# A 32-group fused attention and state-space kernel: the calls of every engine's loop in another order

## The chip, the cores and the metric

The kernel runs on one core of one Trainium2 chip. The metric is the time of one execution on the device in microseconds (us), given as the median of several runs. One further execution was taken with the profiler; all rows below come from that one.

## What is computed

The input is x and a context, 64 sequences of 128 positions by 256 features each, in f32. Three layers follow one another for each sequence:

```python
# 1: attention with 16 heads of 16, queries masked, then add and layernorm
q, k, v = relu(x @ Wq + bq), relu(ctx @ Wk + bk), relu(ctx @ Wv + bv)
x = layernorm(softmax(where(m, q @ k.T / 4, 1e-9)) @ v + x) * gamma + beta
# 2: a state-space block, 8 heads of 64, state 128, a causal convolution of 4 taps
z, xBC, dt = split(rms(x) @ in_proj_w); xBC = silu(conv(xBC)); dt = softplus(dt + dt_bias)
h = h * exp(dt * A) + (dt * xh) B.T;  y = h @ C + D_skip * xh      # a scan over the positions
x = x + rms(y * silu(z)) @ out_proj_w
# 3: cross attention on the same context, 8 heads of 32, then the residual
x = x + (softmax(where(pad, -1e9, layernorm(x) @ Wq1 @ (ctx @ Wk1).T / sqrt(32))) @ (ctx @ Wv1)) @ Wo
```

The state-space part is done as a masked matrix product within each sequence: the scan forms the decay matrix L, TensorE forms C times B, and y is XH times L.

## The kernel before, in words

Two sequences (b = 0, 1) make a group g; there are 32 groups. The program is written engine by engine. Each engine has a set of small helper functions, one for each step of the work of a group, and a loop over s in which they are called in an order that is written out by hand. A call such as cp(s - 3, 0) works on group s - 3 and does nothing when that group does not exist, so the loop is a software pipeline: up to six groups are in flight on one engine. Semaphores join the engines; every helper waits for the counts that it needs, and an engine runs its list strictly in order. The calls on VectorE, ScalarE and GpSimd count their own iterations: only the order on each engine matters, not that s has the same value.

PSUM has eight banks (tiles called bank). The table USES lists in which order TensorE's calls use which bank; the function bank() finds from it what the call must wait for, which is the reader of the last use of that bank.

TensorE's calls (lines 286 to 696) are of three sorts. **Full-array products** take all 128 rows and columns. The projections q, k, v, cp (six of them), z are single-pass products of a value split in a high and a low part (helper proj3, line 294; v in L330, L335); k1, q1 (L535), v1 (L573), o (L522, L523) and wp (L635) are two-record f32 products; gm is L486, dp L445. **Transposes** by the identity: nt, ht, ot, bx, tC (helper turn, L397), tn (L367), bd (L456). **Part-array products** use a part of the rows or columns and stand four (or two) to the array: sA (L354), sT (L387, closed by four products L391) and sC (L593, L597) take 32 rows; av (L411, 8 records a call) and oC (L622, 16 records a call) take 32 columns, y (L508, 16 records a call) 64 columns.

What the steps of a group do, in their order: ScalarE's split_x and split_c and GpSimd's lo_x and lo_c (L1453, L1458) split the inputs; q, k, v, with the results copied out by qe, ke, ve on ScalarE and masked by qm on GpSimd. sA gives the scores for the row maxima (mA on VectorE, L707; nm, L719 and L721), tn and nt_ turn them, sT forms the scores again, transposed, with the maxima subtracted, eA (ScalarE, L1188) takes the exponential, av applies it to V, oa copies, ot transposes, rc and xo (VectorE) divide, xr (GpSimd) adds x. The layernorm is bs, bg, xs, x2 on VectorE with the power rs (L1482) on GpSimd. The rms norm of the second layer is n1 (ScalarE), nr (GpSimd, a power, L1491), nx (ScalarE); nt, nh, nl transpose and split it. dp, d0, de, dc, dq, dd, da, bd, dk form the step sizes and decays; dk's result goes to a DRAM scratch and comes back spread over the partitions (dec_out and dec_in on SyncE, tile DB). cp, ac, tap (L848), th, xc make the convolution; z, zt, sz the gate; bx, xhe, xd and dx the operands; gm the product of C and B. scan (VectorE, L872) makes L out of DB, lg (L881) multiplies it by gm's result, y multiplies by XH, yd (L900) adds; ga (GpSimd, L1518), qq, s2_ gate and square; o projects out, r1 and r2 (a power, L1533), hh (L917) norm and add. hs, hg (L930), hr (GpSimd, a power, L1542), hm (VectorE, L937), hx (ScalarE, L1224, tile xh) are the next layernorm, ht (L397, bank from xh) transposes its result, q1 and k1 project, sC, mC, eC, rC, nC, tC, pC, oC, oT, wp and fin are the cross attention and the last residual. L, SZ, XH, DX, SQ, OA and Q1T are single tiles, the others rings of 2 to 5.

SyncE issues all transfers of the loop, in order, with waits of its own: the loads of a coming group, the decay round trip and the store of a finished one. Four late weight loads, and on VectorE and GpSimd the preparation of the second layer's weights (late(), later()), are put into an early iteration.

## Time and profile before

| | |
|---|---|
| median of 3 runs | 1472.45 us (1471.77 to 1473.89) |
| the profiled execution | 1475.54 us, from its first to its last instruction 1473.7 |
| mean granted TensorE clock in it | 0.979 |
| busy: TensorE, VectorE, ScalarE, GpSimd | 1379.9, 1238.6, 1097.1, 922.4 us |
| instructions | 42007, of them 15112 matrix products |

Busy time is the time in which an engine executes anything. Products on TensorE overlap, so that the distance between the starts of two products is what each costs, not the duration of one; the ends are modelled. A row of the timeline may merge instructions of the same line that follow one another; the brackets give the idle time before it and who ended it. "issue" means that nothing the profile shows was waited for.

### The profile page before, as it was taken

What the parts mean: (1) busy time and instruction counts of PE and PEld (TensorE: products, weight loads), DVE (VectorE), ACT (ScalarE), POOL (GpSimd) and SP (SyncE); (2) the same over time, 40 slices, a digit from 0 to 9 for tenths busy, and PEclk for the clock granted to TensorE, in tenths of its full rate; (3) what the DMA queues carried; (4) which work ended last, traced back from release to release, by engine and by line L of the source; (5) the groups of instructions that cost most, each with busy time, mean ns of one, the idle gap of its engine ahead of it and who ended that gap; (6) DMA issues with size and microseconds to landing.
All of it is one profiled execution on the core that took longest, in us unless ns stands there. A gap on an engine that the chain in (4) does not pass through costs nothing. (4 is left out here: it accounts for less than half of the span.)

```text
span 1473.7 us, 42007 instructions
## 1 busy us (share of the span) xinstructions
PE 1379.9 (94%) x15112; PEld 1175.2 (80%) x15112; DVE 1238.6 (84%) x3050; ACT 1097.1 (74%) x3300; POOL 922.4 (63%) x1125
## 2 busy tenths in 40 slices
...
DMA packets 41132, 86.91 MB, mean 59 GB/s; under 512 B 5728, under 2 KB 10976, under 8 KB 40928
## 3 DMA queue, kind: packets, MB, share of 16 engines
...
q14 instruction: 81, 0.66, 0.1%
...
## 5 line engine op out<-in xcount | busy, mean ns | idle before, releaser
L848 DVE SCALAR_TENSOR_TENSOR ACC<-bank,cw,ACC 128x250 f32<-128x250 f32 (+2 forms) x576 | 271.2, 472 | 25.2 <-ACT ACC L1278 19.2
L1518 POOL TENSOR_TENSOR Y<-Y,SZ 128x512 f32<-128x512 f32 x64 | 140.6, 2197 | 202.2 <-DVE Y L900 202.2
L294 PE MATMUL bank<-xnT,wnl 128*128 128x256 f32 x640 | 202.1, 316 | 1.5 <-ACT PC L1351 0.7
L1188 ACT ACTIVATE PTA<-bank 128x512 f32<-128x512 f32 x256 | 136.3, 603 | 80.1 <-PE bank L391 80.1
L1351 ACT ACTIVATE PC<-bank,stc 128x128 f32<-128x128 f32 x512 | 183.0, 415 | 7.3 <-DVE stc L957 4.8
L294 PE MATMUL bank<-xnL,wnh 128*128 128x256 f32 x640 | 179.5, 280 | 0.0
L294 PE MATMUL bank<-xnT,wnh 128*128 128x256 f32 x640 | 179.3, 280 | 0.0
L707 DVE TENSOR_REDUCE sta<-bank 128x4 f32<-128x512 f32 x256 | 165.7, 679 | 4.2 <-PE bank L354 4.2
L872 DVE TENSOR_TENSOR_SCAN L<-DB,id 128x1024 f32<-128x1024 f32 x64 | 146.1, 2283 | 0.0
L294 PEld LDWEIGHTS bank<-xnT,wnl 128*128 128x128 f32 x640 | 121.0, 189 | 29.4 <-issue 26.2
L1548 POOL TENSOR_TENSOR PC<-PC,stc 128x512 f32<-128x512 f32 x128 | 133.3, 1042 | 10.3 <-DVE stc L964 10.3
L1351 ACT ACTIVATION_READ_ACCUMULATOR PC<-bank,stc 128x1 f32 x512 | 130.6, 255 | 0.0
L1278 ACT ACTIVATE ACC<-bank,cw 128x256 f32<-128x256 f32 x192 | 111.6, 581 | 20.6 <-PE bank L294 19.6
L522 PE MATMUL bank<-wout,Y 128*128 128x256 f32 x512 | 122.5, 382 | 1.9 <-POOL SQ L1526 1.9
L294 PEld LDWEIGHTS bank<-xnL,wnh 128*128 128x128 f32 x640 | 121.6, 190 | 0.0
L294 PEld LDWEIGHTS bank<-xnT,wnh 128*128 128x128 f32 x640 | 121.1, 189 | 0.0
L1363 ACT ACTIVATE PTC<-bank 128x512 f32<-128x512 f32 x128 | 77.7, 609 | 55.9 <-PE bank L397 52.7
L522 PEld LDWEIGHTS bank<-wout,Y 128*128 128x128 f32 x512 | 95.4, 191 | 14.4 <-issue 2.3
L957 DVE TENSOR_REDUCE stc<-bank 128x4 f32<-128x512 f32 x128 | 82.1, 683 | 16.8 <-PE bank L597 16.8
L387 PE MATMUL bank<-QT,KT 32*128 32x128 f32 x2048 | 77.7, 289 | 19.7 <-DVE sta L707 10.0
L937 DVE SCALAR_TENSOR_TENSOR stb<-stb 128x1 f32<-128x1 f32 x64 | 35.6, 557 | 71.5 <-POOL stb L1542 71.5
L1491 POOL TENSOR_TENSOR stn<-stn,mhalf 128x1 f32<-128x1 f32 x64 | 91.6, 1430 | 5.3
...
## 6 DMA issues: line engine op xcount, KB each, us to landing
...
```

Of the source, the lines that this page charges most:

```text
L294: mm = e.matmul(t[:, c0:c0 + T], wt[:, k, m:m + 128], x[:, k, :], start=(n == 0), stop=(n == 5))
L522: e.matmul(t[:, 0:256], Y[b][:, kk * 128:(kk + 1) * 128], wout[:, kk, :], start=(kk == 0), stop=(kk == 3))
L707: e.tensor_reduce(sta[ns % 4][:, 4 * j:4 * j + 4], t[:, :].rearrange("p (i k) -> p i k", i=4), AX_X, ALU.max, negate=True).then_inc(s_mA, 1)
L848: e.scalar_tensor_tensor(out=w, in0=t[:, 0:T].rearrange("p (b t) -> p b t", b=NB)[:, :, 0:125 + k], scalar=cw[:, c, k:k + 1], in1=w, op0=A ...
L872: e.tensor_tensor_scan(L[:, :, :].rearrange("p h t -> p (h t)"), DB[b][:, :], id8[:, :, :].rearrange("p h t -> p (h t)"), 0.0, ALU.mult, A ...
L957: e.tensor_reduce(stc[g % 4][:, 4 * i:4 * i + 4], t[:, :].rearrange("p (i k) -> p i k", i=4), AX_X, ALU.max, negate=True).then_inc(s_mC, 1)
L1188: e.activation(PTA[n % 4][:, :, :], t[:, :].rearrange("p (i k) -> p i k", i=4), ACT.Exp).then_inc(s_eA, 1)
L1278: e.activation(ACC[n % 3][:, :, :], t[:, 0:T].rearrange("p (b t) -> p b t", b=NB), ACT.Identity, bias=cw[:, c, 4:5], scale=cw[:, c, 3:4]). ...
L1351: op = e.activation(PC[n % 5][:, p, :], t[:, p * 128:(p + 1) * 128], ACT.Exp, bias=stc[g % 4][:, 4 * i + p:4 * i + p + 1], accum_out=stc[g ...
L1491: e.tensor_tensor(w, w, mhalf[:, :], ALU.pow).then_inc(s_nr, 1)
L1518: e.tensor_tensor(cv(Y[b][:, :]), cv(Y[b][:, :]), SZ[:, :, b * 128:(b + 1) * 128], ALU.mult).then_inc(s_ga, 1)
L1548: e.tensor_tensor(PC[n % 5][:, :, :], PC[n % 5][:, :, :], stc[g % 4][:, 16 + 4 * i:20 + 4 * i].unsqueeze(2).to_broadcast([128, 4, 128]), A ...
```

## The change

The calls of all five loops are put into another order, with other distances between groups, and the bank of every use is assigned anew. No helper function is changed, and every group has the same instructions as before. The loop has two iterations more, of which the first four give TensorE no work. The late weight loads are issued in iteration 6 instead of 4 of SyncE's list, and late() on VectorE runs in iteration 5 instead of 2 of its list; on GpSimd late() and later() stay in iterations 1 and 2. In the diff, the calls of an iteration are written side by side, with nothing left out but the middle of USES.

```diff
 USES = [
-    (("tn", 0, 2), 4), (("nt", 0, 3), 6), (("ht", 1, 5), 7), (("y", 0, 4), 3), (("sT", 0, 2), 4), (("sT", 1, 2), 7),
...
+    (("sT", 0, 6), 3), (("sT", 1, 6), 7), (("sT", 2, 6), 4), (("sT", 3, 6), 0), (("y", 1, 8), 2), (("tC", 3, 9), 3),
...
 ]
-STEPS = NG + 9
+STEPS = NG + 11
@@ the calls of one iteration, sync @@
-                if s == 4:
+                if s == 6:
-dec_in(s-7, 1) dec_in(s-7, 0) load_m(s-4) load_c(s-4) store(s-9) load_u(s-6) load_t(s-5) load_x(s-3)
-dec_out(s-6)
+load_t(s-7) dec_in(s-9, 1) load_x(s-5) load_c(s-5) dec_out(s-8) store(s-11) load_m(s-5) load_u(s-7)
+dec_in(s-8, 0)
@@ the calls of one iteration, tensor @@
-tn(s-2, 0) nt(s-3, 0) ht(s-5, 1) y(s-4, 0) sT(s-2, 0) q1(s-5, 0) q1(s-5, 1) bx(s-4, 1) gm(s-4, 1) dp(s-3, 0)
-tn(s-2, 1) sC(s-5, 0) av(s-2, 0) av(s-2, 1) av(s-2, 2) cp(s-3, 0) y(s-4, 1) cp(s-3, 1) av(s-2, 3) k1(s-3, 0)
-k1(s-3, 1) o(s-4, 0) tC(s-5, 0) q(s-1, 0) ot(s-2, 0) cp(s-3, 2) sT(s-2, 1) cp(s-3, 3) bd(s-3, 0) cp(s-3, 4)
-q(s-1, 1) z(s-3, 0) av(s-2, 4) av(s-2, 5) av(s-2, 6) tC(s-5, 1) av(s-2, 7) cp(s-3, 5) tC(s-5, 2) k(s-1, 0)
-ot(s-2, 1) k(s-1, 1) o(s-4, 1) sA(s-1, 0) tC(s-5, 3) z(s-3, 1) oC(s-5, 0) oC(s-5, 1) v(s-1, 0) bx(s-3, 0)
-sA(s-1, 1) v1(s-3, 0) ht(s-4, 0) gm(s-3, 0) wp(s-5, 0)
+sT(s-6, 0) y(s-8, 1) tC(s-9, 3) cp(s-7, 0) dp(s-7, 0) q(s-5, 1) cp(s-7, 1) av(s-6, 0) av(s-6, 1) oC(s-9, 0)
+av(s-6, 2) oC(s-9, 1) av(s-6, 3) tn(s-6, 1) o(s-8, 1) ot(s-6, 0) cp(s-7, 2) ht(s-8, 0) cp(s-7, 3) sT(s-6, 1)
+bd(s-7, 0) cp(s-7, 4) z(s-7, 0) av(s-6, 4) av(s-6, 5) av(s-6, 6) av(s-6, 7) ht(s-8, 1) cp(s-7, 5) q1(s-8, 0)
+q1(s-8, 1) ot(s-6, 1) k1(s-6, 0) sC(s-8, 0) wp(s-9, 0) v(s-5, 0) bx(s-7, 0) k1(s-6, 1) gm(s-7, 0) tC(s-8, 0)
+z(s-7, 1) sA(s-5, 0) y(s-7, 0) tC(s-8, 1) k(s-4, 0) k(s-4, 1) q(s-4, 0) sA(s-5, 1) bx(s-7, 1) tC(s-8, 2)
+tn(s-5, 0) v1(s-6, 0) gm(s-7, 1) nt(s-6, 0) o(s-7, 0)
@@ the calls of one iteration, vector @@
-                if s == 2:
+                if s == 5:
-mA(s-2, 4) hm(s-5, 1) lg(s-4, 0) fin(s-6, 0) mA(s-2, 5) mA(s-2, 6) mA(s-2, 7) nl(s-3, 0) nl(s-3, 1) nm(s-2,
-1) yd(s-4, 0) scan(s-4, 1) lg(s-4, 1) d0(s-3, 0) d0(s-3, 1) mC(s-5, 0) mC(s-5, 1) mC(s-5, 2) dc(s-3, 0)
-dc(s-3, 1) dc(s-3, 2) yd(s-4, 1) tap(s-3, 0) rC(s-5, 0) dc(s-3, 3) dc(s-3, 4) mC(s-5, 3) tap(s-3, 1) dc(s-3,
-5) dc(s-3, 6) rC(s-5, 1) dc(s-3, 7) dc(s-3, 8) tap(s-3, 2) dc(s-3, 9) dc(s-3, 10) kk1(s-3, 0) kk1(s-3, 1)
-tap(s-3, 3) r1(s-4, 0) tap(s-3, 4) rC(s-5, 2) dc(s-3, 11) hh(s-4, 0) rc(s-2, 0) xc(s-3, 0) rC(s-5, 3)
-tap(s-3, 5) xo(s-2, 0) tap(s-3, 6) tap(s-3, 7) xc(s-3, 1) dk(s-3, 0) bs(s-2, 0) bg(s-2, 0) tap(s-3, 8)
-xs(s-2, 0) tap(s-3, 9) hs(s-4, 0) tap(s-3, 10) tap(s-3, 11) xc(s-3, 2) x2(s-2, 0) sz(s-3, 0) hg(s-4, 0)
-xc(s-3, 3) tap(s-3, 12) tap(s-3, 13) tap(s-3, 14) tap(s-3, 15) rc(s-2, 1) xo(s-2, 1) tap(s-3, 16) tap(s-3,
-17) xc(s-3, 4) hm(s-4, 0) bs(s-2, 1) bg(s-2, 1) r1(s-4, 1) xs(s-2, 1) xc(s-3, 5) hh(s-4, 1) mA(s-1, 0)
-hs(s-4, 1) mA(s-1, 1) hg(s-4, 1) x2(s-2, 1) mA(s-1, 2) mA(s-1, 3) sz(s-3, 1) scan(s-3, 0) nm(s-1, 0)
+dc(s-6, 2) tap(s-6, 3) tap(s-6, 4) tap(s-6, 5) xc(s-6, 0) dc(s-6, 3) dc(s-6, 4) dc(s-6, 5) hm(s-7, 0)
+dc(s-6, 6) dc(s-6, 7) r1(s-7, 1) dc(s-6, 8) dc(s-6, 9) dc(s-6, 10) xc(s-6, 1) hh(s-7, 1) rc(s-5, 0) hs(s-7,
+1) hg(s-7, 1) dc(s-6, 11) xo(s-5, 0) tap(s-6, 6) tap(s-6, 7) hm(s-7, 1) dk(s-6, 0) tap(s-6, 8) tap(s-6, 9)
+bs(s-5, 0) bg(s-5, 0) tap(s-6, 10) xs(s-5, 0) tap(s-6, 11) xc(s-6, 2) tap(s-6, 12) x2(s-5, 0) tap(s-6, 13)
+tap(s-6, 14) sz(s-6, 0) xc(s-6, 3) tap(s-6, 15) tap(s-6, 16) tap(s-6, 17) xc(s-6, 4) rc(s-5, 1) xo(s-5, 1)
+xc(s-6, 5) mC(s-7, 0) mC(s-7, 1) kk1(s-5, 0) mC(s-7, 2) fin(s-8, 0) rC(s-7, 0) scan(s-6, 0) rC(s-7, 1)
+lg(s-6, 0) mC(s-7, 3) kk1(s-5, 1) rC(s-7, 2) bs(s-5, 1) sz(s-6, 1) bg(s-5, 1) mA(s-4, 0) mA(s-4, 1) mA(s-4,
+2) yd(s-6, 0) xs(s-5, 1) mA(s-4, 3) x2(s-5, 1) nm(s-4, 0) mA(s-4, 4) mA(s-4, 5) mA(s-4, 6) mA(s-4, 7)
+rC(s-7, 3) scan(s-6, 1) lg(s-6, 1) r1(s-6, 0) nl(s-5, 0) nl(s-5, 1) nm(s-4, 1) yd(s-6, 1) hh(s-6, 0) hs(s-6,
+0) hg(s-6, 0) d0(s-5, 0) d0(s-5, 1) tap(s-5, 0) tap(s-5, 1) tap(s-5, 2) dc(s-5, 0) dc(s-5, 1)
@@ the calls of one iteration, scalar @@
-pC(s-6, 0) qe(s-2, 0) da(s-4, 0) ac(s-4, 2) th(s-4, 1) eA(s-3, 4) eA(s-3, 5) eA(s-3, 6) ac(s-4, 3) eA(s-3,
-7) ac(s-4, 4) th(s-4, 2) qq(s-5, 1) zt(s-4, 0) th(s-4, 3) qe(s-2, 1) pC(s-6, 1) oa(s-3, 1) pC(s-6, 2)
-ac(s-4, 5) th(s-4, 4) ke(s-2, 0) ke(s-2, 1) th(s-4, 5) hx(s-5, 0) pC(s-6, 3) split_x(s-1) zt(s-4, 1) oT(s-6,
-0) n1(s-3, 0) n1(s-3, 1) ve(s-2, 0) xhe(s-4, 0) nx(s-3, 0) split_c(s-1) he(s-5, 0) nx(s-3, 1) v1e(s-4, 0)
-hx(s-5, 1) nt_(s-2, 0) he(s-5, 1) nh(s-3, 0) nh(s-3, 1) eA(s-2, 0) eA(s-2, 1) eA(s-2, 2) eA(s-2, 3) q1e(s-5,
-0) q1e(s-5, 1) xhe(s-4, 1) nt_(s-2, 1) de(s-3, 0) de(s-3, 1) qq(s-4, 0) de(s-3, 2) eC(s-5, 0) ac(s-3, 0)
-dq(s-3, 0) eC(s-5, 1) oa(s-2, 0) ac(s-3, 1) eC(s-5, 2) eC(s-5, 3) th(s-3, 0) dd(s-3, 0)
+de(s-7, 2) ac(s-7, 1) qe(s-5, 1) dq(s-7, 0) th(s-7, 0) oT(s-9, 0) oa(s-6, 0) th(s-7, 1) v1e(s-7, 0) hx(s-8,
+0) nt_(s-6, 1) dd(s-7, 0) he(s-8, 0) ac(s-7, 2) da(s-7, 0) split_x(s-4) ac(s-7, 3) eA(s-6, 4) eA(s-6, 5)
+eA(s-6, 6) hx(s-8, 1) eA(s-6, 7) th(s-7, 2) ac(s-7, 4) he(s-8, 1) zt(s-7, 0) th(s-7, 3) oa(s-6, 1) ac(s-7,
+5) q1e(s-8, 0) q1e(s-8, 1) th(s-7, 4) n1(s-6, 0) th(s-7, 5) eC(s-8, 0) eC(s-8, 1) xhe(s-7, 0) ve(s-5, 0)
+eC(s-8, 2) split_c(s-4) zt(s-7, 1) eC(s-8, 3) nx(s-6, 0) pC(s-8, 0) pC(s-8, 1) ke(s-4, 0) ke(s-4, 1) qe(s-4,
+0) n1(s-6, 1) qq(s-7, 0) nt_(s-5, 0) nx(s-6, 1) xhe(s-7, 1) pC(s-8, 2) nh(s-6, 0) nh(s-6, 1) eA(s-5, 0)
+eA(s-5, 1) pC(s-8, 3) eA(s-5, 2) ac(s-6, 0) eA(s-5, 3) qq(s-7, 1) de(s-6, 0) de(s-6, 1)
@@ the calls of one iteration, gpsimd @@
-dx(s-3, 0) xr(s-2, 1) r2(s-4, 1) rs(s-2, 1) nr(s-2, 0) nr(s-2, 1) lo_x(s) hr(s-4, 1) xd(s-3, 0) ga(s-3, 0)
-xd(s-3, 1) dx(s-3, 1) s2_(s-3, 0) ga(s-3, 1) nC(s-4, 0) lo_c(s) nC(s-4, 1) r2(s-3, 0) nC(s-4, 2) xr(s-1, 0)
-rs(s-1, 0) s2_(s-3, 1) qm(s, 0) nC(s-4, 3) qm(s, 1) hr(s-3, 0)
+qm(s-1, 0) r2(s-4, 1) qm(s-1, 1) hr(s-4, 1) xr(s-2, 0) rs(s-2, 0) nr(s-2, 0) dx(s-3, 0) xr(s-2, 1) nC(s-4,
+0) xd(s-3, 0) nC(s-4, 1) lo_c(s) lo_x(s) nC(s-4, 2) rs(s-2, 1) ga(s-3, 0) nr(s-2, 1) s2_(s-3, 0) xd(s-3, 1)
+nC(s-4, 3) dx(s-3, 1) r2(s-3, 0) ga(s-3, 1) hr(s-3, 0) s2_(s-3, 1)
```

## Rows read from the trace of the kernel before

**Rows 1.** The page: its first line and TensorE's busy time.

```profile
span 1473.7 us, 42007 instructions
...
PE 1379.9 (94%) x15112; PEld 1175.2 (80%) x15112; DVE 1238.6 (84%) x3050; ACT 1097.1 (74%) x3300; POOL 922.4 (63%) x1125
```

**Rows 2.** Busy time by window: core, window, length, then each engine busy (instructions), clock, DMA share.

```profile
0.00:72.00 72.00, 38.83 (x359) 30.79 (x360) 36.21 (x82) 25.86 (x63) 32.75 (x57) 0.76 0.32 102
700.00:743.50 43.50, 42.18 (x474) 36.12 (x473) 37.94 (x95) 34.10 (x104) 28.29 (x35) 1.00 0.19 60
1403.00:1473.70 70.70, 54.08 (x441) 42.71 (x441) 39.06 (x98) 41.94 (x150) 34.73 (x41) 0.88 0.08 27
```

**Rows 3.** TensorE's timeline: start, busy, line, tiles, count, idle time before.

```profile
715.26 0.86 PE L411 MATMUL bank<-PTA,V 128*32 128x128 f32 x24
716.05 0.39 PE L294 MATMUL bank<-xnT,wnl 128*128 128x256 f32 x1
716.28 0.28 PE L294 MATMUL bank<-xnL,wnh 128*128 128x256 f32 x1
716.40 0.28 PE L294 MATMUL bank<-xnT,wnh 128*128 128x256 f32 x1
...
716.75 0.28 PE L294 MATMUL bank<-xnT,wnh 128*128 128x256 f32 x1
716.96 1.09 PE L508 MATMUL bank<-L,XH 128*64 128x128 f32 x16
...
718.86 0.43 PE L411 MATMUL bank<-PTA,V 128*32 128x128 f32 x8
719.22 1.99 PE L535 MATMUL bank<-cU,wk 128*128 128x256 f32 x8
...
731.30 0.66 PE L397 MATMUL bank<-ident,PC 128*128 128x128 f32 x4
731.89 0.42 PE L411 MATMUL bank<-PTA,V 128*32 128x128 f32 x8
...
740.43 1.08 PE L622 MATMUL bank<-PTC,V 128*32 128x128 f32 x32
741.44 0.50 PE L330 MATMUL bank<-vbias,onesr 128*128 128x512 f32 x1
```

**Rows 4.** TensorE's timeline, where it is idle in that step.

```profile
706.89 0.41 PE L397 MATMUL bank<-ident,xh 128*128 128x128 f32 x2 [0.90 <-ACT xh L1224]
...
708.79 1.12 PE L387 MATMUL bank<-QT,KT 32*128 32x128 f32 x29 [0.41 <-issue]
```

**Rows 5.** VectorE's timeline of the same step.

```profile
699.48 2.28 DVE L872 TENSOR_TENSOR_SCAN L<-DB,id 128x1024 f32<-128x1024 f32 x1
...
705.06 0.99 DVE L937 SCALAR_TENSOR_TENSOR stb<-stb 128x1 f32<-128x1 f32 x1 [2.42 <-POOL stb L1542]
...
707.70 1.87 DVE L707 TENSOR_REDUCE sta<-bank 128x4 f32<-128x512 f32 x3
...
713.45 1.22 DVE L881 TENSOR_TENSOR L<-L,bank 128x1024 f32<-128x1024 f32 x1
...
737.16 0.15 DVE L937 SCALAR_TENSOR_TENSOR stb<-stb 128x1 f32<-128x1 f32 x1
...
743.01 2.28 DVE L872 TENSOR_TENSOR_SCAN L<-DB,id 128x1024 f32<-128x1024 f32 x1
```

**Rows 6.** The list of waits, the wait of L937.

```profile
DVE stb L937 <- POOL stb L1542: 71.5, 31, 3.0
```

**Rows 7.** GpSimd's timeline of the same step.

```profile
699.49 2.63 POOL L1491 TENSOR_TENSOR stn<-stn,mhalf 128x1 f32<-128x1 f32 x1
...
704.16 0.21 POOL L1540 TENSOR_SCALAR stb<-stb 128x1 f32<-128x1 f32 x1
704.46 0.57 POOL L1542 TENSOR_TENSOR stb<-stb,mhalf 128x1 f32<-128x1 f32 x1
704.99 1.04 POOL L1509 TENSOR_TENSOR XH<-XH,dtt 128x512 f32<-128x512 f32 x1
```

More of the change, by code:

```diff
@@ new lines, in tensor @@
+                av(s - 6, 3)
+                tn(s - 6, 1)
+                o(s - 8, 1)
+                ot(s - 6, 0)
+                cp(s - 7, 2)
+                ht(s - 8, 0)
+                cp(s - 7, 3)
+                sT(s - 6, 1)
+                bd(s - 7, 0)
+                cp(s - 7, 4)
+                z(s - 7, 0)
+                av(s - 6, 4)
+                av(s - 6, 5)
+                av(s - 6, 6)
+                av(s - 6, 7)
+                ht(s - 8, 1)
+                cp(s - 7, 5)
@@ new lines, in tensor @@
+                q1(s - 8, 0)
+                q1(s - 8, 1)
+                ot(s - 6, 1)
+                k1(s - 6, 0)
+                sC(s - 8, 0)
+                wp(s - 9, 0)
+                v(s - 5, 0)
+                bx(s - 7, 0)
+                k1(s - 6, 1)
+                gm(s - 7, 0)
+                tC(s - 8, 0)
+                z(s - 7, 1)
+                sA(s - 5, 0)
+                y(s - 7, 0)
+                tC(s - 8, 1)
+                k(s - 4, 0)
+                k(s - 4, 1)
@@ new lines, in vector @@
+                dc(s - 6, 4)
+                dc(s - 6, 5)
+                hm(s - 7, 0)
+                dc(s - 6, 6)
+                dc(s - 6, 7)
+                r1(s - 7, 1)
+                dc(s - 6, 8)
+                dc(s - 6, 9)
+                dc(s - 6, 10)
+                xc(s - 6, 1)
+                hh(s - 7, 1)
+                rc(s - 5, 0)
+                hs(s - 7, 1)
+                hg(s - 7, 1)
+                dc(s - 6, 11)
+                xo(s - 5, 0)
+                tap(s - 6, 6)
@@ new lines, in vector @@
+                tap(s - 6, 15)
+                tap(s - 6, 16)
+                tap(s - 6, 17)
+                xc(s - 6, 4)
+                rc(s - 5, 1)
+                xo(s - 5, 1)
+                xc(s - 6, 5)
+                mC(s - 7, 0)
+                mC(s - 7, 1)
+                kk1(s - 5, 0)
+                mC(s - 7, 2)
+                fin(s - 8, 0)
+                rC(s - 7, 0)
+                scan(s - 6, 0)
+                rC(s - 7, 1)
+                lg(s - 6, 0)
+                mC(s - 7, 3)
```

410 lines of the change are left out of this document (171 added, 239 removed), and 20 rows, old and new, of the table USES.

## The prediction

> **What bounds the kernel now.** I read the page first: TensorE is busy 1379.9 of 1473.7 us, 94%, and the engine after it, VectorE, 1238.6 us [rows 1]. Then one step of the loop: VectorE's first scan of a step starts at 699.48 and the next one at 743.01 [rows 5], so a step takes 43.5 us, and in a stretch of that length TensorE is busy 42.2, VectorE 37.9, ScalarE 34.1 and GpSimd 28.3 us at the full granted clock, 1.00 [rows 2]. Filling and draining take the first 72 us (38.8 busy) and the last 70.7 (54.1 busy) [rows 2]; the 1331 us between them hold the starts of some thirty steps. So TensorE's own list of work sets the step, plus whatever holds it up. Both parts are read from its timeline.
>
> TensorE's work contains something that busy time hides. The single-pass projections (L294) start 0.12 us apart (716.28 to 716.40). Where a part-array product stands before or after one, it is more: 0.21 from the last projection to the product (716.75 to 716.96), and 0.23 from the first projection behind it to the second (716.05 to 716.28). Eight part-array products alone between full ones take 0.36 us (718.86 to 719.22), but twenty-four in a row take 0.79 (715.26 to 716.05) [rows 3]: a further sixteen cost 0.43, eight of them 0.215. So a lone group costs 0.36 - 0.215 = 0.145 of its own, 0.09 at the full product ahead and 0.11 at the full product behind: **0.345 us for each separate run**. Where the neighbour is a transpose the way back is cheaper: four transposes between two such groups take 0.59 (731.30 to 731.89) against 4 x 0.11, so 0.15 for both sides of them together [rows 3].
>
> TensorE also waits at one place in each step: 0.90 us for ScalarE's xh (706.89), and, the queue then being empty, another 0.41 ahead of sT (708.79) [rows 4], 1.31 together. Followed back: VectorE's hm (L937) waits 2.42 us, 31 times [rows 5, 6]; it waits for the power at 704.46 on GpSimd, which stands there behind a power of 2.63 us, and takes 0.57 itself [rows 7], since GpSimd ran beside the scan that began at 699.48; and hm itself then takes 0.99 instead of 0.15 (737.16 [rows 5]), while GpSimd's multiplication of 704.99 runs beside it.
>
> **The change, part by part.**
>
> Part-array groups that stand together. Counting the 55 calls of a step, runs of part-array calls between full ones are ten before: {y0 sT0}, {sC av0-2}, {y1}, {av3}, {sT1}, {av4-6}, {av7}, {sA0}, {oC0 oC1}, {sA1}. After it seven: {sT0 y1}, {av0 av1 oC0 av2 oC1 av3}, {sT1}, {av4-7}, {sC}, {sA0 y0}, {sA1}. Priced: av3 joins, -0.345. av7 joins, and its neighbour was a transpose group: -0.30. oC joins av: oC alone takes 1.01 for thirty-two, of which 0.145 goes (740.43 to 741.44 [rows 3]), -0.345. y1 comes beside sT0 in place of y0, and y0 beside sA0: one run fewer, but the products are of different shapes and I let each keep its own 0.145, so only -0.20. sC is parted from av: +0.20. Sum **-0.99**. Moreover six of the seven runs are now followed by transposes (tC, tn, bd, ht, tC, bx) where eight of ten were followed by projections or the like: up to 5 x 0.055 = 0.27 more, of which I take 0.1, because a transpose just pays for a single product. Together 1.1 us a step (ends 0.8, if unlike shapes and alternating calls gain nothing, and 1.25), in all 32 groups: **-35 us**.
>
> The rule against this in the Trainium skill ("TensorE: Matmul & The Clock Gate", Part 3, The mechanism) is that a weight load overlaps with products in flight only when it goes to another row group; all the av and oC products use all rows, so by it each would wait for its own load and nothing would be gained by standing side by side; the step would lose only the waits. It is a rival below. The trace speaks against it: 0.027 us between starts in a row of av.
>
> The waits. In the new order VectorE has hm0 sixteen places behind hg0, across the loop's end, and hm1 five behind hg1: dc11, xo0, tap6, tap7 and then hm1, about 1.4 us, in which GpSimd needs 0.8 (0.21 and 0.57, rows 7) if it is free; and on GpSimd hr1 now stands fourth, no longer behind the powers of nr and lo_x. ht0 and ht1 on TensorE no longer stand together ahead of y: ht1 comes after av7, some 3.5 us behind sT1. So the 1.31 us should go. What is late next? I laid the new lists beside one another with the durations of the rows. The nearest ring: sA1 ends, VectorE does mA4 to mA7, rC3, scan1, lg1 (three mA in 1.87, scan 2.28, lg 1.22 [rows 5]: 6.1 us), then y1 may start; TensorE meanwhile has bx1, tC2, tn0, v1, gm1, nt, o0, sT0, 6.8 us. A margin of 0.5 after two crossings. Others (nt behind nx1, oT behind oC1, d0 behind dp) have 0 to 0.6. New waits are therefore between 0 and the old 1.31; I take 0.45, near zero since every margin that I can work out is positive, but not zero since they are small. Gain 0.86 us in the 29 full steps: **-25 us**. VectorE allows it: with its busy 37.9 and all its idle time except the 2.42 it would need at most 43.5 - 2.4 = 41.1 a step, against a TensorE step of 43.5 - 1.1 - 0.86 = 41.5.
>
> Edits with nothing to pay. Banks (USES): the same eight; the new place of each is covered by the margins above. SyncE: DMA engines are busy a fifth of the time [rows 2]; the decay transfer (dec_out, then dec_in 0) still starts behind dk and has some 11 us on VectorE's list until scan0; dec_in 1 is one iteration later but scan1 is 12 us behind scan0. If it were late, each microsecond would stand in front of scan and lg and soon of y. GpSimd: moved past its own power instructions, 28.3 busy, so there is room. The ends: two iterations more in the loop, but the first four are empty; from the first k to the last wp there are 4.8 steps against 4.6. The late weights (late on VectorE) come after the maxima instead of ahead of them, and late on GpSimd now stands before qm of group 0. I put that at 0, with 8 us either way.
>
> **The sum.** -35 - 25 = -60. The profiled execution took 1475.5 us (its span 1473.7 and some 1.8 around it), so 1415.5; the median of the runs shown is 3.1 lower, 1472.45, so **1413** for the median.
>
> **Rivals.**
> 1. *The waits form again at their old size.* The switches go (-35), but the rings catch TensorE as before, for 1.3 us a step: 1437. For it: several margins of a few tenths, VectorE at 37.9 of 42.4. Against: the one old wait has a clear cause that is gone.
> 2. *Joining gains nothing*, since each product pays for its own weights whatever stands beside it, or since gaps only move: the waits go, -25, 1447. The 0.215 against 0.36 speaks against it.
> 3. *Both fall away*, within 3 us of before: 1470 to 1475.
> 4. *Slower: GpSimd and VectorE block one another and VectorE becomes the bound.* Place: VectorE's hh, hm, x2 and bs, each behind a small power on GpSimd, with the two scans of a step. A power beside a scan took 2.1 us more than alone, and hm beside a multiplication 0.84 more [rows 5, 7]. These are eight places in a step. With its 41.1 (everything but the one wait) it loses to the old order as soon as these meetings add more than 2.4 us; two lost powers (4.2) less half a microsecond of cover each make the step 44.0, +0.5 x 31: 1488. Against: GpSimd has 13 us of room and the powers stand early in its list. The Trainium skill ("SBUF — State Buffer", Who interferes with whom) has the cause: a VectorE instruction with two SBUF inputs and a GpSimd one that reads SBUF exclude each other for the whole instruction. By that rule only the timing of the two lists counts, which no row of before shows for the new lists.
>
> **How the numbers follow.** The forecast, 1398 to 1430: 0.50. Better than that, with no new wait and the ends better: 0.05. Rival 1 (to 1450): 0.23. Rival 2: 0.05. Rival 3: 0.05. Rival 4: 0.12. A run of this kernel can be told from no change at about 0.2%, 3 us. Faster 0.83, same 0.05, slower 0.12. Low end: 1.25 x 32 + 1.31 x 29 + 6 at the ends = 84, 1389. The high end takes in rivals 1 and 2 and half of the way to 3: 1460; left out are 0.17.
>
> **What would show it.** Step: scan to scan 41.2 to 41.9 us. Switches: TensorE busy 1345 or so; the row av, av, oC, av, oC, av (64 products) in one piece of some 1.95 us with no step of 0.36; four to six transposes behind a run at 0.15 over their own time in all. Waits: the idle before ht, 26 us in total now, under 5; hm's wait for GpSimd under 15 us in total; new TensorE waits of under 0.5 us a step, first at y1 (for L) or nt (for xn). Wrong if: TensorE's busy time stays over 1370 (rival 2), if the busy time falls but waits of 1.3 us a step stand elsewhere (rival 1), or if VectorE is over 94% busy or waits for GpSimd over 2.4 us a step (rival 4). A longer stretch ahead of the first cp than 80 us would make the ends the step that failed.

## The result: 1428.5 us, 3.0% less, and the profile after

| | before | after |
|---|---|---|
| median, same chip | 1473.07 us | 1428.51 us (1427.62 to 1431.83) |
| ratio | | 0.9702, 95% interval 0.9684 to 0.9721 |
| first instruction to last, profiled | 1473.7 us | 1426.0 us |
| up to the first cp | 71.8 us | 58.5 us |
| 31 steps, first cp to last cp | 1331.3 us | 1294.4 us |
| behind the last cp | 70.6 us | 73.2 us |

The change makes the kernel 3% faster, inside the predicted range and 15 us above the predicted number. The last three lines are read from the starts of cp(…, 0) on TensorE (the expectations below put the first of them 0.2 to 0.3 us earlier): of the 47.7 us gained, 36.9 are in the steps and 10.8 at the two ends.

The page of after, its first line, busy times and the granted clock, against [rows 1]:

```profile
span 1426.0 us, 42008 instructions
...
PE 1329.9 (93%) x15112; PEld 1160.4 (81%) x15112; DVE 1267.2 (89%) x3050; ACT 1089.3 (76%) x3300; POOL 891.7 (63%) x1125
...
PEclk9999999999999999999999999999999999999997
```

Busy time by window of after (window, length, each engine busy with its count, clock, DMA share), one step and the fill, against [rows 2]:

```profile
700.00:741.84 41.84, 40.52 (x472) 35.55 (x471) 38.17 (x93) 33.23 (x101) 27.19 (x34) 1.00 0.21 60
0.00:36.00 36.00, 16.40 (x166) 13.53 (x167) 20.86 (x36) 14.02 (x31) 24.36 (x44) 1.00 0.57 188
36.00:77.00 41.00, 31.48 (x379) 25.07 (x378) 33.33 (x96) 25.14 (x66) 14.42 (x23) 1.00 0.14 44
```

The step shown takes 41.84 us (VectorE's scan0 at 704.88, then 746.7), not 43.5. It is one of the shorter ones: the middle steps take 41.8 to 43.0, 42.2 in the mean. TensorE is busy 40.52 of the 41.84, down from 42.18 of 43.50, and VectorE a little more. So the busy time fell as forecast, but 1.3 us of each step is idle still.

TensorE's timeline of after, the two waits of a step and the rows that the change made, against [rows 3, 4]:

```profile
699.53 1.10 PE L535 MATMUL bank<-cU,wk 128*128 128x256 f32 x4 [0.51 <-DMA cU<-in_cT]
...
706.62 0.39 PE L486 MATMUL bank<-XC 128*128 128x128 f32 x2
708.12 0.63 PE L397 MATMUL bank<-ident,PC 128*128 128x128 f32 x4 [1.11 <-POOL PC L1548]
...
727.30 0.64 PE L411 MATMUL bank<-PTA,V 128*32 128x128 f32 x16
727.76 0.62 PE L622 MATMUL bank<-PTC,V 128*32 128x128 f32 x16
728.20 0.40 PE L411 MATMUL bank<-PTA,V 128*32 128x128 f32 x8
728.42 0.62 PE L622 MATMUL bank<-PTC,V 128*32 128x128 f32 x16
728.86 0.40 PE L411 MATMUL bank<-PTA,V 128*32 128x128 f32 x8
729.19 0.33 PE L367 MATMUL bank<-ident,NM 128*128 128x128 f32 x1
```

The merged row (av, av, oC, av, oC, av: 64 products) takes 1.89 us from 727.30 to the transpose at 729.19, with no step of 0.36 in it. The old wait of 0.90 for xh is gone, and there are two new ones: 1.11 us at the transpose tC0 for GpSimd's normalised rows PC, and 0.51 at k1 for a transfer. The list of waits of after (engine, line, waited for: us in total, times, longest) says how often:

```profile
PE bank L397 <- POOL PC L1548: 36.1, 33, 2.1
...
PE bank L535 <- DMA cU<-in_cT: 5.1, 9, 1.2
...
PE bank L397 <- ACT xh L1224: 3.9, 2, 3.5
```

The wait at ht for xh was 26.3 us over the run and is 3.9 now, and hm's wait for GpSimd, 71.5 us [rows 6], is 2.1. The cause of the new wait is on the other two engines. VectorE's and GpSimd's timelines of after:

```profile
704.20 0.68 DVE L970 TENSOR_TENSOR X<-bank,X 128x512 f32<-128x512 f32 x1
704.80 0.17 DVE L964 RECIPROCAL stc<-stc 128x4 f32<-128x4 f32 x1
704.88 2.26 DVE L872 TENSOR_TENSOR_SCAN L<-DB,id 128x1024 f32<-128x1024 f32 x1
...
707.25 1.22 DVE L881 TENSOR_TENSOR L<-L,bank 128x1024 f32<-128x1024 f32 x1
```

```profile
705.05 2.93 POOL L1548 TENSOR_TENSOR PC<-PC,stc 128x512 f32<-128x512 f32 x1 [2.62 <-DVE stc L964]
...
708.94 1.03 POOL L1548 TENSOR_TENSOR PC<-PC,stc 128x512 f32<-128x512 f32 x1
```

rC0 (0.17 us, L964) gives GpSimd what nC0 needs, but the scan starts right behind it at 704.88, and nC0 at 705.05 then takes 2.93 us instead of the 1.03 of the next one. tC0 stands behind it. Over the whole run these multiplications took 1.49 us each where they had taken 1.04; the group of L1548 in before and in after (count, then busy time and mean ns of one, then the idle time before):

```profile
L1548 POOL TENSOR_TENSOR PC<-PC,stc 128x512 f32<-128x512 f32 x128 | 133.3, 1042 | 10.3 <-DVE stc L964 10.3
```

```profile
L1548 POOL TENSOR_TENSOR PC<-PC,stc 128x512 f32<-128x512 f32 x128 | 191.1, 1494 | 78.0 <-DVE stc L964 78.0
```

And the transfer: SyncE's timeline of after, and the chain of waits of after where it passes through:

```profile
692.90 0.32 SPq L256 DMA_DIRECT2D dec_scratch<-decT  x1
693.27 0.42 SPq L270 DMA_DIRECT2D out_x<-X  x1
693.74 0.43 SPq L250 DMA_DIRECT2D QM<-qm_rows  x1
694.60 0.33 SPq L244 DMA_DIRECT2D cU<-in_cT  x1
```

```profile
694.60 4.80 DMA cU<-in_cT
```

load_u stands behind dec_out, which waits for VectorE's dk, so cU is issued at 694.60 and lands 4.8 us later, at 699.40; k1 has by then waited 0.51. In some steps it waits up to 1.2 us, which is why the steps of after are uneven (41.8 to 43.0) where those of before were even (43.5).

### The profile page after: what moved, and what is told of

The parts are those of the page before. It is cut to its first block, busy times and chain, and to the rows that moved or that the text cites. A ratio compares the mean times of both kernels' runs of the same rounds, so it can differ in the third digit from the quotient of the medians.

```text
span 1426.0 us, 42008 instructions
## 1 busy us (share of the span) xinstructions
PE 1329.9 (93%) x15112; PEld 1160.4 (81%) x15112; DVE 1267.2 (89%) x3050; ACT 1089.3 (76%) x3300; POOL 891.7 (63%) x1125
## 4 chain that ended last, share of the span: by engine, by line
PE 72%; DVE 11%; POOL 8%; issue 4%; DMA 3%; ACT 1%; SPq 1%; POOLq 0%; DVEq 0%; ACTq 0%
PE bank L294 19%; PE bank L397 9%; PE bank L522 8%; POOL PC L1548 6%; PE bank L535 5%; PE bank L354 5%; PE bank L508 4%; PE bank L387 4%; PE bank L573 4%; PE bank L411 4%; DVE stc L957 3%; DMA cU<-in_cT 3%; PE bank L593 2%; PE bank L622 2%; PE bank L445 2%
## 5 line engine op out<-in xcount | busy, mean ns | idle before, releaser
L1548 POOL TENSOR_TENSOR PC<-PC,stc 128x512 f32<-128x512 f32 x128 | 191.1, 1494 | 78.0 <-DVE stc L964 78.0
L1188 ACT ACTIVATE PTA<-bank 128x512 f32<-128x512 f32 x256 | 142.2, 599 | 82.3 <-PE bank L391 80.1
L294 PE MATMUL bank<-xnT,wnl 128*128 128x256 f32 x640 | 199.2, 311 | 0.3 <-DVE xnL L783 0.3
L707 DVE TENSOR_REDUCE sta<-bank 128x4 f32<-128x512 f32 x256 | 160.8, 681 | 8.1 <-PE bank L354 5.6
L1489 POOL TENSOR_SCALAR stn<-stn 128x1 f32<-128x1 f32 x64 | 15.2, 238 | 173.2 <-ACT junk L1207 173.2
L1509 POOL TENSOR_TENSOR XH<-XH,dtt 128x512 f32<-128x512 f32 x64 | 107.3, 1677 | 24.4 <-ACT XH L1295 24.4
L397 PE MATMUL bank<-ident,PC 128*128 128x128 f32 x512 | 83.4, 287 | 39.7 <-POOL PC L1548 36.1
L1351 ACT ACTIVATION_READ_ACCUMULATOR PC<-bank,stc 128x1 f32 x512 | 112.5, 220 | 0.0
L397 PEld LDWEIGHTS bank<-ident,PC 128*128 128x128 f32 x512 | 56.4, 143 | 57.0 <-issue 47.3
L1518 POOL TENSOR_TENSOR Y<-Y,SZ 128x512 f32<-128x512 f32 x64 | 81.8, 1279 | 21.3 <-DVE Y L900 21.1
```

The costliest lines, as they stand in the source:

```text
L294: mm = e.matmul(t[:, c0:c0 + T], wt[:, k, m:m + 128], x[:, k, :], start=(n == 0), stop=(n == 5))
L397: mm = e.transpose(t[:, c0 + i * 128:c0 + (i + 1) * 128], src(i), ident[:, :])
L707: e.tensor_reduce(sta[ns % 4][:, 4 * j:4 * j + 4], t[:, :].rearrange("p (i k) -> p i k", i=4), AX_X, ALU.max, negate=True).then_inc(s_mA, 1)
L1188: e.activation(PTA[n % 4][:, :, :], t[:, :].rearrange("p (i k) -> p i k", i=4), ACT.Exp).then_inc(s_eA, 1)
L1351: op = e.activation(PC[n % 5][:, p, :], t[:, p * 128:(p + 1) * 128], ACT.Exp, bias=stc[g % 4][:, 4 * i + p:4 * i + p + 1], accum_out=stc[g ...
L1509: e.tensor_tensor(hv(XH[:, :]), hv(XH[:, :]), dtt[g % 3][:, b * 8:b * 8 + 8].unsqueeze(2).to_broadcast([128, 8, 64]), ALU.mult).then_inc(s ...
```

## The experiments

The theory before the experiments: fewer separate runs of part-array products make TensorE's list 1.4 us a step shorter; the old wait ended because hr1 moved forward on GpSimd; it was replaced by a wait that comes from scan0's place; the cU wait comes from load_u's place on SyncE; and the fill is shorter because late() stands elsewhere on VectorE. The rival for each is that the piece does nothing alone, and that the new overall order has the gain. Five of the twelve kernels are edits to the kernel before (b), seven to the kernel after (a, s). Every edit moves calls within the list of one engine; nothing is computed otherwise. "Own" below is TensorE's time with its waits taken out: the distance between the first products of two calls that follow one another, averaged over the middle steps; where a call waits, the distance of the same pair, or of a like pair, without a wait is put in its place. The kernels were measured in four groups, the last three on three different chips, each beside the kernel before, which took 1473.07, 1473.23, 1473.86 and 1475.79 us in them (after; b1 to b123; a1, a2, sa, sb; a3, a4, a42, b27). A difference of medians from different groups can therefore be out by some 3 us; the distances within the traces don't have this error.

### Part-array products beside their like, alone

```diff
 # b1, before, TensorE
-av(s-2,2) cp(s-3,0) y(s-4,1) cp(s-3,1) av(s-2,3)
+av(s-2,2) av(s-2,3) cp(s-3,0) y(s-4,1) cp(s-3,1)
...
-tC(s-5,1) av(s-2,7) cp(s-3,5)
+av(s-2,7) tC(s-5,1) cp(s-3,5)
```

> The kernel before with two moves on TensorE alone: av3 next to av2, av7 next to av6, so eight separate runs of part-array products in place of ten. Theory (a separate run costs 0.345 us, 0.30 beside a transpose): -0.645 us a step, some -20 us, 1453. Rival (each product pays for its own weights, or the gap only moves): within 3 us of before, 1473. Should the step be set by the ring over GpSimd that makes TensorE wait at ht1, the wait grows by what is saved and the time also stays.

Measured: 1456.32 us, ratio 0.9884 (0.9867 to 0.9902), 17 us less. That looks like the forecast 0.645 a step, and is not. The step falls by 0.6, but the own time only by 0.30: moving av7 gives 0.335, and moving av3, all in all, costs 0.04. The other 0.3 is the wait at ht1, which this order happens to shrink from 26.3 to 17.2 us. TensorE's timeline of this kernel, where av3 has gone from between cp1 and k1, and the wait:

```profile
710.89 0.28 PE L294 MATMUL bank<-xnT,wnh 128*128 128x256 f32 x1
711.18 1.99 PE L535 MATMUL bank<-cU,wk 128*128 128x256 f32 x8
```

```profile
PE bank L397 <- ACT xh L1224: 17.2, 29, 1.1
```

cp1, a single-pass product, and k1, a two-record one, are now neighbours, and the step between them is 0.26 to 0.29, where two products of the single-pass kind are 0.12 apart. So this pair takes some 0.15 of what av3 gave back; at the three places that the move touches it still gains 0.07. It loses that and more where nothing was edited: another 0.13 appears between o0 and tC0 (0.24 instead of 0.11). The same 0.13 is there in b123 and absent in b2 and b27, so it comes with av3's move; why is open. That the two products are of different kinds is not what costs: k1 to o1 in before, also a single-pass product with a two-record one behind it, are 0.12 apart, and cp5 to q1 in after 0.135. The next kernels hold the two moves apart:

```diff
 # b27, before, TensorE and GpSimd: b1's second move alone, with b2's (below)
-tC(s-5,1) av(s-2,7) cp(s-3,5)
+av(s-2,7) tC(s-5,1) cp(s-3,5)
 # GpSimd
-nr(s-2,0) nr(s-2,1) lo_x(s) hr(s-4,1)
+hr(s-4,1) nr(s-2,0) nr(s-2,1) lo_x(s)
```

> The kernel before with hr early on GpSimd (no wait left on TensorE in the full steps, 1428.1 us) and only the second of b1's moves, av7 next to av6, where the two neighbours that come together are transposes and a single-pass projection. Theory (a removed run pays in full where the full products that then meet follow one another at no cost, and nothing where they do not, as cp1 and k1): -0.30 x 31 = -9 us, 1419, so that the av3 merge is worth about nothing or less. Rival (each removed run is worth the same): b1's pair was worth 0.2 us a step without waits, so half of it, -3 us, 1425.

Measured: 1420.70 us, ratio 0.9621 (0.9596 to 0.9646). Against b2 alone (1428.12) the av7 move brings 7.4 us, 0.26 a step: most steps of b27 take some 41.6, those of b2 41.83, and with both of b1's moves (b123, below) 41.65. So moving av3 brings nothing, or takes 0.06, when TensorE is never idle; moving av7 brings 0.26 and not the 0.30 that was priced.

```diff
 # sb, after, TensorE: the merged row parted again
-cp(s-7,1) av(s-6,0) av(s-6,1) oC(s-9,0) av(s-6,2)
+av(s-6,0) av(s-6,1) oC(s-9,0) cp(s-7,1) av(s-6,2)
...
-av(s-6,5) av(s-6,6) av(s-6,7) ht(s-8,1)
+av(s-6,5) av(s-6,6) ht(s-8,1) av(s-6,7)
```

> The changed kernel with two moves on TensorE: cp1 into the middle of the row of av and oC, ht1 between av6 and av7. Two more separate runs of part-array products, of like shapes. Theory: +0.345 and +0.20 to 0.30 us a step, together some +19 us, 1447. Rival (what stands beside what costs nothing by itself): within 3 us of 1428.5.

Measured: 1449.33 us, ratio 0.9829 (0.9814 to 0.9843), 20.8 us more than after. The own time rises by 0.57 a step and the waits stay as they were. It is spread over the sides: 0.09 at q1, 0.10 at cp1, 0.11 behind oC0, 0.11 at av6, 0.17 at ht1. This is the clean measurement of a joining: two separate runs more, +0.57, 0.29 each, where 0.345 and 0.30 had been priced.

```diff
 # sa, after, TensorE: unlike part-array calls parted
-sT(s-6,0) y(s-8,1) tC(s-9,3)
+sT(s-6,0) tC(s-9,3) y(s-8,1)
```

> The changed kernel with one move on TensorE: the transposes tC3 between sT0 (32 rows) and y1 (64 columns) in place of behind y1. Theory (unlike part shapes side by side save only the two sides of the full product): +0.15 to 0.20 us a step, +5 to 6 us, 1434. Rival (unlike shapes gain nothing from standing together): within 2 us of 1428.5. If they gain as much as like ones: +9 us or more.

Measured: 1462.0 us, ratio 0.9915 (0.9900 to 0.9931), 33.5 us more: far more than any price of a switch. tC3, now one microsecond earlier, has to wait in each step. TensorE's and ScalarE's timelines of this kernel:

```profile
738.47 0.50 PE L391 MATMUL bank<-NT,onesr 32*128 32x512 f32 x4
739.72 0.66 PE L397 MATMUL bank<-ident,PC 128*128 128x128 f32 x4 [0.75 <-ACT PTA L1188]
```

```profile
739.07 1.09 ACT L1188 ACTIVATE PTA<-bank 128x512 f32<-128x512 f32 x2 [2.51 <-PE bank L391]
```

What it waits for is a bank. In USES tC3 takes bank 3, which the first product group of sT0 has just filled, and ScalarE's first eA has to read it; its own input, nC3 on GpSimd, ends at 738.98 and was not the last. In after y1 stood between the two and covered this. The list of waits has 21.8 us for it, 29 times. So the time of this run doesn't answer the question, but its distances do, with the wait taken out: sT0 to tC3 set to the 1.34 us of sT1 and the transpose behind it in after, the three calls sT0, tC3, y1 take 2.95 us up to cp0, where sT0, y1, tC3 take 2.77. That is an estimate of 0.18 for the parting, within the forecast 0.15 to 0.20, and it agrees with the trace of after: from sT0's closing products to y1 is 0.40 us, the same as from sT0 to a full product before, and y1's own products take as long as behind a full one. Of a run of unlike shapes only the full product's two sides are saved.

### What ended the old wait

```diff
 # b2, before, GpSimd
-rs(s-2,1) nr(s-2,0) nr(s-2,1) lo_x(s) hr(s-4,1)
+rs(s-2,1) hr(s-4,1) nr(s-2,0) nr(s-2,1) lo_x(s)
```

> The kernel before with one move on GpSimd alone: hr of the second sequence ahead of the two powers of nr and of lo_x. Theory (the waits of 0.90 and 0.41 us at ht1 and sT come from hr standing behind a power that runs beside the scan): VectorE's hm no longer waits (71 us in total before), TensorE's wait before ht goes, -1.31 x 29 = -38 us, 1435. Rival (the next ring holds TensorE at once): under a third of it, -12 us, with the same idle time at another call.

Measured: 1428.12 us, ratio 0.9693 (0.9678 to 0.9708): one call moved on one engine that is 63% busy brings as much as the whole change. Busy time by window, the waits of VectorE, and GpSimd's timeline of this kernel:

```profile
700.00:741.83 41.83, 41.82 (x473) 36.04 (x472) 37.15 (x95) 34.00 (x104) 28.38 (x35) 1.00 0.18 62
```

```profile
DVE stb L937 <- POOL stb L1542: 3.9, 2, 2.9
```

```profile
718.90 0.35 POOL L1540 TENSOR_SCALAR stb<-stb 128x1 f32<-128x1 f32 x1 [1.40 <-DVE stb L930]
719.34 0.57 POOL L1542 TENSOR_TENSOR stb<-stb,mhalf 128x1 f32<-128x1 f32 x1
```

TensorE is busy 41.82 of 41.83 us. hm's wait falls from 71.5 us [rows 6] to 3.9. The old order had one fault, and its price was the step's 43.5 less 41.83, 1.7 us, more than the 1.31 that its idle rows show: TensorE's busy time falls too, from 1379.9 to 1362.8 us, with the same products; by the distances of its calls nearly 0.2 us a step of it is in its own time. TensorE's list is the same in both, so this too goes with the wait; the largest piece, 0.08, lies between ht1 and y0, directly behind the place of the wait. How the wait lengthens them no run tells.

### The fill

```diff
 # b3, before, VectorE                       # a3, after, VectorE
-if s == 2: late()   (ahead of mA(s-2,4))     -if s == 5: late()
+if s == 2: late()   (behind nm(s-2,1))       +if s == 4: late()
```

> The kernel before with one move on VectorE alone: late(), the preparation of the second layer's weights, after the maxima of group 0 in place of ahead of them, as the changed kernel has it. Theory (this is where the 13 us came from by which the first cp starts earlier after the change, 58.2 us in place of 71.6, since sT of group 0 waited 10.0 us for a maximum behind late): first cp 10 us earlier, -10 us in all, 1463. Rival (the fill is set by loads and by GpSimd): first cp within 2 us of before, time within 3.

> The changed kernel with one edit: late() on VectorE in iteration 4 in place of 5, so ahead of the maxima of group 0, as before the change. Theory (its place explains most of the earlier first cp): first cp 7 to 10 us later than 58.2 us, total +7 to +10, 1437. Rival (the fill is shorter for other reasons, as the projections ahead of it): within 3 us.

Measured: b3 1466.27 us, ratio 0.9951 (0.9933 to 0.9969); its first cp starts at 64.5 us instead of 71.8. a3 1437.33 us, ratio 0.9741 (0.9719 to 0.9763), 8.8 more than after; its first cp starts at 69.5 instead of 58.5. So late()'s place is worth 7 us of the fill in the old order and 11 in the new one (7 and 9 in the medians), which is half to four fifths of the 13.4 by which the fill is shorter. The old order gives 3 us less than its forecast of 10, and what makes the rest of the fill shorter is open. Busy time by window, 36 to 77 us, of before, b3, a3:

```profile
36.00:77.00 41.00, 31.67 (x317) 24.92 (x318) 17.73 (x51) 19.93 (x52) 16.41 (x28) 0.69 0.05 14
```

```profile
36.00:77.00 41.00, 30.66 (x282) 25.66 (x283) 23.41 (x71) 19.99 (x52) 18.55 (x32) 0.75 0.05 15
```

```profile
36.00:77.00 41.00, 34.66 (x372) 27.58 (x372) 20.59 (x57) 23.18 (x61) 11.48 (x18) 0.81 0.07 21
```

With TensorE busy for about the same 31 us, it gets through 379 products in after and 317 in before: the granted clock is 1.00 in after, 0.69 in before. In the time ahead of it (0 to 36 us) TensorE is busy 16.4 us in after and 12.2 in before. That alone does not decide it: b3 was busy 17.3 us ahead of its stretch at 0.75, and a3 only 9.8 ahead of its stretch at 0.81. What sets the clock of the fill stays open.

### The old kernel with all three

b123 is b1, b2 and b3 together.

> The kernel before with the three moves together. Theory (three separate causes): the sum, -20 - 38 - 10 = -68, some 1405, which would be below the changed kernel. Rival (the gains hide one another, since one ring or VectorE's 37.9 us of work bounds what is left): 1430 or more, near the changed kernel's 1428.5.

Measured: 1417.28 us, ratio 0.9615 (0.9598 to 0.9632). Alone the three moves bring 17, 45 and 7 us, 69 together; at once they bring 56. Of the missing 13, 9 are the part of the wait at ht1 by which b1 shrinks it (26.3 to 17.2), since b2 takes the wait away whole. b123 is faster than after by 11 us. Four calls moved in the old order get more than the complete new order, whose work on TensorE is a whole microsecond a step shorter (40.65 against 41.64) and is spent again on waits.

### The new waits

```diff
 # a1, after, VectorE
-rC(s-7,0) scan(s-6,0) rC(s-7,1) lg(s-6,0) mC(s-7,3) kk1(s-5,1)
+rC(s-7,0) mC(s-7,3) kk1(s-5,1) rC(s-7,1) scan(s-6,0) lg(s-6,0)
```

> The changed kernel with one move on VectorE: the first scan after mC3, kk1 and rC1 in place of directly after rC0. Theory (the new wait of 1.1 us at tC0 comes from nC0 on GpSimd, released by rC0 and then held up beside the scan, 2.9 us in place of 1.0): nC0 back to about 1.04 us, the wait at tC0 gone, up to -1.1 x 29 = -32 us, 1397; half of it if y0 becomes late, since lg moves back by 1 us. Rival (VectorE, 89% busy, sets the step): within 5 us of the changed kernel's 1428.5.

Measured: 1515.15 us, ratio 1.0268 (1.0232 to 1.0304), 87 us slower than after. The wait meant to go went, and a larger one came. The waits of TensorE, a row of its timeline and a window of this kernel:

```profile
PE bank L354 <- DVE L L881: 74.0, 30, 2.8
...
PE bank L397 <- POOL PC L1548: 2.8, 3, 2.1
```

```profile
758.84 1.60 PE L354 MATMUL bank<-KT,QT 32*128 32x256 f32 x16 [2.47 <-DVE L L881]
```

```profile
700.00:744.80 44.80, 42.14 (x463) 37.06 (x464) 37.64 (x91) 31.97 (x100) 27.64 (x34) 0.92 0.16 44
```

GpSimd is free of the scan, and tC0's wait falls from 36.1 to 2.8 us. But the bank that gm0 fills is read by lg0, and the call that takes this bank next is sA0. The timeline of VectorE shows how late lg0 comes:

```profile
752.27 0.17 DVE L964 RECIPROCAL stc<-stc 128x4 f32<-128x4 f32 x1
752.36 0.66 DVE L957 TENSOR_REDUCE stc<-bank 128x4 f32<-128x512 f32 x1
754.34 0.42 DVE L946 TENSOR_TENSOR K1T<-bank,keep 128x256 f32<-128x256 f32 x1 [1.32 <-PE bank L535]
...
754.76 2.70 DVE L872 TENSOR_TENSOR_SCAN L<-DB,id 128x1024 f32<-128x1024 f32 x1
757.57 1.22 DVE L881 TENSOR_TENSOR L<-L,bank 128x1024 f32<-128x1024 f32 x1
```

Behind rC0 at 752.27 stand now mC3 and kk1, which waits 1.32 us for TensorE's k1, and the scan starts at 754.76, 2.4 us later than it would have; sA0 then waits 2.47, and 74.0 in all. Over the step the granted clock is 0.92, with TensorE idle 2.7 of 44.8 us. The low clock stands behind the wait, where most of the stretch is at the lower of its two levels, 1.2 of 2.4 GHz:

```profile
758.80:763.00 4.20, 4.16 (x37) 3.15 (x37) 3.46 (x8) 0.51 (x2) 3.71 (x5) 0.59 0.28 77
```

In the 13.8 us ahead of this window and the 26 behind it the clock is 1.00. The calls in it, sA0, y0 and tC1, take 1.53, 1.91 and 0.65 us to the next one, where they take 1.08, 1.03 and 0.41 in after: 1.6 us in this step. So the 2.7 us that a step is longer (44.9 against 42.2 in the mean) are about half the larger wait and half the clock behind it. This chain (scan0, lg0, bank, sA0) was not among the rings that I had worked out.

```diff
 # a4, after, VectorE
-mC(s-7,2) fin(s-8,0) rC(s-7,0) scan(s-6,0)
+mC(s-7,2) rC(s-7,0) fin(s-8,0) scan(s-6,0)
```

> The changed kernel with one move on VectorE: rC0 ahead of fin in place of behind it, so nC0 on GpSimd is released 0.6 us before the scan starts instead of with it. Theory (nC0 held up beside the scan makes TensorE's wait at tC0): nC0 well under 2.9 us, the wait of 36 us in total mostly gone, up to -0.9 x 29 = -26 us, 1402. Against it stands what a1_scan_late showed, that sA0 waits for the bank which lg0 frees: scan itself may lose 0.4 us beside nC0, and then sA0, without the wait at tC0, comes 1.1 us earlier and meets lg0's end; in that case about two thirds, 1410. Rival (VectorE sets the step): same as 1428.5.

Measured: 1404.75 us, ratio 0.9517 (0.9494 to 0.9539), 24 us less than after with one call moved by one place. VectorE's timeline, GpSimd's and the waits of TensorE of this kernel:

```profile
736.44 0.18 DVE L964 RECIPROCAL stc<-stc 128x4 f32<-128x4 f32 x1
736.54 0.66 DVE L970 TENSOR_TENSOR X<-bank,X 128x512 f32<-128x512 f32 x1
737.11 2.77 DVE L872 TENSOR_TENSOR_SCAN L<-DB,id 128x1024 f32<-128x1024 f32 x1
```

```profile
736.70 1.04 POOL L1548 TENSOR_TENSOR PC<-PC,stc 128x512 f32<-128x512 f32 x1 [1.88 <-DVE stc L964]
```

```profile
PE bank L354 <- DVE L L881: 9.0, 28, 0.4
```

rC0 now stands 0.67 us ahead of the scan, so that nC0 starts at 736.70, ahead of it, and takes 1.04. The scan, started while nC0 runs, takes 2.77 instead of 2.26. tC0 no longer waits; sA0 waits a little instead (9.0 us in all, up to 0.4 a time), which is what is late next. The shortest steps are 41.0 us; with cU still late, as in after, they go up to 41.9, 41.3 in the mean.

```diff
 # a2, after, SyncE
-load_c(s-5) dec_out(s-8) store(s-11) load_m(s-5) load_u(s-7) dec_in(s-8,0)
+load_c(s-5) load_u(s-7) dec_out(s-8) store(s-11) load_m(s-5) dec_in(s-8,0)
```

> The changed kernel with one move on SyncE: the load of cU ahead of the decay's store. Theory (cU lands a little late for k1, behind a store that waits for dk; this makes some steps 42.1 to 43.0 us long where most take 41.8): steps even at 41.8, -8 us, 1420. Rival (the uneven steps come from elsewhere): same within 3 us.

Measured: 1422.35 us, ratio 0.9651 (0.9635 to 0.9667), 6 us less than after. The waits for cU are gone and every step in the middle is 41.7 to 42.0.

### The best version

a42 is a4 and a2 together.

> The changed kernel with a4_rc_before_fin's move and a2_cu_early's together. Theory (two causes, one for even and one for uneven steps): the gain of a4 and 6 us more, 1396 to 1404. Rival: one hides the other, no better than a4 alone.

Measured: 1398.88 us, ratio 0.9478 (0.9446 to 0.9510): 5.2% less than before and 30 us less than after, the two gains added. The steps in the middle are 41.0 to 41.1. Busy time by window, one step:

```profile
700.00:740.70 40.70, 40.39 (x472) 35.72 (x470) 38.98 (x95) 33.49 (x103) 26.21 (x35) 1.00 0.19 63
```

TensorE is busy 40.39 of 40.70 us and VectorE 38.98.

## Why the prediction was right and wrong, point by point

**The bound.** Right. TensorE's list sets the step before and after, and what it waits for comes on top. (The sum, 1415.5 less 3.1, is 1412.4; 1413 is half a microsecond off.)

**The switches: −1.1 us a step.** Right in kind, too small: the own time fell from 42.03 to 40.65 us, by 1.38, or 44 us over 32 groups where 35 had been forecast. It is not right in each term. Joining like with like is worth 0.29 a run (sb), 0.26 for av7 (b27), against the 0.345 and 0.30 priced. The term for av3 was wrong as a rule: it had left out what stands at the place that a run has left, and there (b1, b123) it brings nothing. In the new order cp1 is followed by av0, and no such pair arises. The parting of unlike shapes is worth 0.18 by the distances of sa, as priced. The term that was too small is the transposes behind a run, of which 0.1 had been taken of a possible 0.27. The distances give this estimate: a run costs 0.09 at its entry (0.21 from the full product, where two single-pass ones are 0.12 apart); at its end it costs 0.19 if a single-pass product follows (0.20 to it and 0.23 to the one behind it, against twice 0.12), and 0.09 if a transpose does. Ten entries less seven are 0.27 a step; eight ends of the dear kind and two of the cheap one, less one and six, are 0.97. That is 1.24 of the 1.38, of which the transposes make some 0.5. Single-pass and two-record products do not meet less often after the change, so they are not the rest, and 0.14 stays open.

**The rule of the Trainium skill** ("TensorE: Matmul & The Clock Gate", Part 3, The mechanism), by which all-row products would gain nothing by standing together: this kernel goes against it. The merged row's 64 products take 1.89 us, 0.030 each, while their weight loads take about 0.11 each (0.109 for av, 0.112 for oC in after), so the loads do overlap, though all of them use all rows; and sb, which parts them, costs 0.57 a step. (The rule taken from that section is its list of what overlaps; the text above that list also lets a load into the background weight buffer run ahead.) Rival 2 is out.

**The waits: −1.31 + 0.45.** The first half right, the second wrong; this is the step that failed. The old wait is gone, for the reason given, and b2 shows the reason alone. But new waits of 1.50 us a step stand in its place: 1.23 at tC0 and 0.27 at k1, by the same measure by which the old one was 1.48. The net gain is none where 25 us had been forecast. So in the steps rival 1 was right, and that the forecast came within 1.1% is in good part luck, since two other terms ran the other way: 9 us more from the switches and 11 from the ends. These terms add up to 55 us, and the profiled executions differ by 47.7: 3.3 of the difference is the last distance from cp0 to cp0, where the pipeline runs out (38.9 us after, 35.65 before), and the rest is mostly that 1.38 is the gain of a middle step, which the first and last groups do not have. The new first wait was sought at y1 or nt, in a ring between VectorE and TensorE. It stood where I had not looked, in nC0 behind scan0: the ring that I had worked out took every duration as it was in the old order, and nC0's 1.04 us was one that the new order itself made 2.93.

**Rival 4** had this mechanism (GpSimd and VectorE exclude each other) but priced it on VectorE's path, to a slowdown. The rule of the Trainium skill behind it ("SBUF — State Buffer", Who interferes with whom) is borne out: of two such instructions that meet, the one that starts second waits for the whole of the first. nC0 behind a scan that started 0.17 before it took 2.93 us, and alone 1.04; with nC0 first (a4) it was the scan that took 2.77 instead of 2.26. The second one is held for nearly all that was left of the first: 1.89 us longer where 2.09 of the scan were left, 0.51 where 0.63 of nC0 were left. VectorE was busy 28.6 us more in all, but not in the scans, which took 2.28 on average before and after. Its rows that grew are nm's first instruction (L719, 0.17 to 0.50 us each) and x2 (L769, 0.47 to 0.70), while hm's fell (0.56 to 0.28). In the step shown one x2 takes 0.92 beside ga on GpSimd, and one L719 0.90 beside dx. So rival 4's price on VectorE was paid in small part too, but VectorE was never the bound (38.2 of 41.84 a step).

**SyncE "with nothing to pay".** Wrong by some 6 us (a2). I had looked at how busy the transfer engines are, a fifth of the time, and not at what stands ahead of load_u in SyncE's list: dec_out, which waits for VectorE. The queue was idle and the load late nonetheless. The decay transfers, which I had named, never were late.

**The ends at 0, 8 either way.** They were −10.8: a fill 13.4 us shorter, a drain 2.6 longer. late()'s place, which I named and then put at nothing, is 7 of it in the old order and 11 in the new.

**What would have shown it.** The merged row of 1.89 is near the forecast 1.95. Scan to scan is 41.84 in the best steps, inside 41.2 to 41.9, but 42.2 in the mean, outside it. TensorE's busy time, 1329.9, is under the 1345; ht and hm are under their bounds (3.9 and 2.1 us); the new waits, 1.50 a step, are over the 0.5 and fit the sign that had been set for rival 1.
